# Attention: six unread products per unit on TensorE in the first five units as well

## What is computed

```python
q = jnp.transpose(q * scale, (0, 2, 1, 3))
...
q = _fq_sym(q, axis=-1)
k = _fq_sym(k, axis=-1)
v = _fq_sym(v, axis=2)
attn = jnp.einsum('bhqd,bhkd->bhqk', q, k)
attn = jax.nn.softmax(attn.astype(jnp.float32), axis=-1)
attn = _fq_unsigned(attn, axis=-1)
out = jnp.einsum('bhqk,bhkd->bhqd', attn, v)
```

## Time and profile before

| | |
|---|---|
| median of three runs | 1748.34 us (1745.9 to 1749.89) |
| profiled execution | 1749.91 us |
| its span | 1748.1 us |
| VectorE busy | 1629.3 us, 93% |
| TensorE matmuls busy | 1534.1 us, 88% |
| ScalarE busy | 1400.3 us, 80% |
| GpSimd busy | 1307.5 us, 75% |
| mean granted clock of TensorE | 0.971 |

### The profile page before, as it was taken

How to read it: one execution, slowest core, us unless ns; L and a number is a source line. 1 busy time by engine, 2 the same in 40 slices (tenths; PEclk the granted TensorE clock), 3 DMA queues, 4 the chain that set the end, 5 groups by cost and what they waited for, 6 DMA issues and landing times.

```text
span 1748.1 us, 34660 instructions
## 1 busy us (share of the span) xinstructions
PE 1534.1 (88%) x13190; PEld 752.2 (43%) x13207; DVE 1629.3 (93%) x2214; ACT 1400.3 (80%) x1354; POOL 1307.5 (75%) x1311
## 2 busy tenths in 40 slices
PE   7999968898898889889889887988888888989986
PEld 3544423444444444444444444444444444433332
DVE  6978889999999999999999999999999999588887
ACT  4578887888898888888888888987888887776874
POOL 1156737889889988988998898898998998553332
PEclk9999978999999999999999999999999998999998
DMA  7578849999868999885898999588897876314223
GB/s 243 198 255 286 282 179 172 167 186 174 153 119 143 182 175 187 177 154 107 140 186 168 179 176 158 112 148 155 151 158 144 160 138 140 79 37 97 60 68 84
DMA packets 721031, 274.22 MB, mean 157 GB/s; under 512 B 675609, under 2 KB 680281, under 8 KB 719586
## 3 DMA queue, kind: packets, MB, share of 16 engines
q1 hardware_dynamic: 719058, 268.81, 74.5%
q0 software_dynamic: 704, 1.62, 0.3%
q10 hardware_dynamic: 1104, 1.57, 0.3%
HBM read 68.21 MB, written 35.95 MB: 60 GB/s over the span
## 4 chain that ended last, share of the span: by engine, by line
DVE 48%; POOL 13%; PE 13%; issue 9%; ACT 2%; DMA 1%; POOLq 0%; DVEq 0%; ACTq 0%
DVE att_scaled L1804 46%; POOL att_probsT L1503 10%; PE att_scores L1233 3%; PE att_ps_o L1253 2%; PE att_scores L1173 2%; PE att_scores L1193 2%; POOL att_low_row L1493 1%; PE att_scores L1234 1%; ACT att_pairs L1330 1%; POOL att_bias_row L1496 1%; PE att_scores L1133 1%; DVE att_v_largest L1773 0%; PE att_ps_v L1253 0%; POOL layer_o_sum L1551 0%; DMA att_pairsT<-att_pairs 0%
## 5 line engine op out<-in xcount | busy, mean ns | idle before, releaser
L1804 DVE TENSOR_SCALAR_CACHE_REDUCE att_scaled<-att_scores,layer_nsq 128x1536 f32<-128x1536 f32 (+1 forms) x768 | 1201.2, 1637 | 13.9 <-PE att_scores L1193 10.8
L1330 ACT ACTIVATE att_pairs<-att_scaled,att_bias_row 128x4096 uint8<-128x4096 f32 x256 | 950.5, 3713 | 118.4 <-DMA att_pairsT<-att_pairs 76.3
L1503 POOL CAST att_probsT<-att_pairsT 128x2048 bf16<-128x2048 uint8 x512 | 953.6, 1891 | 95.2 <-DMA att_pairsT<-att_pairs 83.4
L1193 PE MATMUL att_scores<-first_head_area 96*128 96x512 bf16 x1024 | 297.9, 395 | 94.1 <-DVE att_scaled L1804 79.4
L1193 PE MATMUL att_scores<-att_head_area 96*128 96x512 bf16 x1024 | 289.3, 385 | 65.4 <-DVE att_scaled L1804 62.2
L1152 PEld LDWEIGHTS att_ps_o<-att_v_head,att_probsT 128*128 128x128 bf16 x8192 | 243.0, 96 | 65.0 <-issue 6.5
L1152 PE MATMUL att_ps_o<-att_v_head,att_probsT 128*128 128x32 bf16 x8192 | 245.3, 177 | 2.1 <-ACT layer_o_sum L1321 2.0
L1193 PEld LDWEIGHTS att_scores<-first_head_area 96*128 96x128 bf16 x1024 | 81.4, 99 | 255.4 <-DVE att_scaled L1804 174.9
L1193 PEld LDWEIGHTS att_scores<-att_head_area 96*128 96x128 bf16 x1024 | 79.7, 98 | 214.3 <-DVE att_scaled L1804 153.0
L1133 PE MATMUL att_scores<-att_head_area 96*128 96x512 bf16 x621 | 170.3, 384 | 0.0
L1133 PE MATMUL att_scores<-first_head_area 96*128 96x512 bf16 x570 | 158.1, 387 | 0.0
(11 more groups left out here) (192 smaller groups left out, 1596.7 us busy)
## 6 DMA issues: line engine op xcount, KB each, us to landing
layer_w2T<-ctx_T SPq DMA_DIRECT2D x96, 256.0 KB, 3.8
k_rows<-pre_shared SPq DMA_DIRECT2D x32, 392.0 KB, 2.9
pre_x_in<-in_x_dram SPq DMA_DIRECT2D x32, 256.0 KB, 4.1
kv_weights_ctx_in<-in_ctx_dram SPq DMA_DIRECT2D x32, 256.0 KB, 3.8
ctx_T<-layer_o_sum SPq DMA_DIRECT2D x8, 1024.0 KB, 5.2
pre_w_more<-in_L_ffn_w_dram SPq DMA_DIRECT2D x18, 256.0 KB, 3.4
terns<-pre_q_stage SPq DMA_DIRECT2D x32, 128.0 KB, 3.1
xb<-pre_x_in SPq DMA_DIRECT2D x16, 256.0 KB, 3.3
```

The costliest lines, as they stand in the source:

```text
L1193: last = pe.matmul(buffer[:, x:x + 512], q_head[slot][:, at:at + P], k_head[slot][:, STARTS[j] + x:STARTS[j] + x + 512], start=True, stop= ...
L1330: act.activation(pairs[g % R_BUFS][:, :].bitcast(U8).rearrange("p (c two) -> p two c", two=2), scaled[u][:, :].rearrange("p (two c) -> p t ...
L1503: pool.tensor_copy(probsT[g % C_BUFS][:, parity * HALF:(parity + 1) * HALF, :].rearrange("p k q -> p (k q)"), bytes_now.rearrange("p (n tw ...
L1804: dve.tensor_scalar(scaled[u][:, STARTS[j]:STARTS[j] + WIDTHS[j]], scores[(g * NCH + j) % 2][:, 0:WIDTHS[j]], kept["nsq"][:, g:g + 1], Non ...
```

## The change

In `step`, the condition under which the unread products are issued is widened. After j = 0 they now come in every live unit that has neither a value chunk nor early work; after j = 2 they come in every live unit that has no early work. Units 0 to 3 thus get three products in each place, unit 4 (which has a value chunk after j = 0) gets three after j = 2. In unit 0 the products after j = 0 go to columns 1024 to 1535 of `scores[1]`, ahead of chunk j = 1, which overwrites them.

```diff
@@ -1198,11 +1198,11 @@
                         elif j == 0 and live(g, UNITS):
                             if (g, j) in EARLY_PE:
                                 early_work(*EARLY_PE[g, j])
-                            elif live(g - V_LAG, UNITS):
+                            else:
                                 keep_clock(g - 1, slot, at, 3)
                         if j == 1 and live(g - V_LAG, UNITS):
                             weigh(g - V_LAG)
-                        if j == 2 and live(g - V_LAG, UNITS):
+                        if j == 2 and live(g, UNITS):
                             if (g, j) in EARLY_PE:
                                 early_work(*EARLY_PE[g, j])
                             else:
```

## The result

The changed kernel took 1760.31 us (median of four runs, 1757.39 to 1764.38), against 1749.12 us (1745.9 to 1755.44) for the kernel before beside it: ratio 1.0053, 95% interval 1.003 to 1.0077. It is slower by 0.5%, where 1746.1 us and no difference above 0.2% were forecast. A second comparison, with five runs against 17, gave 1.0082 (1.0064 to 1.0099). The profiled execution after took 1764.38 us, its span is 1762.5.

The account below looks back on a forecast made before the run. VectorE was taken to bound the kernel, with TensorE's low clock delaying it in the first five units. −3.04 + 0.8 = −2.24 us from the median 1748.34 gave 1746.1 us, range 1744.2 to 1749.6.

Parts of the forecast that it names:

- The low clock in units 0 to 4, and its price of 3.04 us: Attention's first five units: TensorE at 1.2 GHz makes VectorE wait for scores, 3.04 us over five units of 4.68.
- The clock rises within unit 0: TensorE in attention's unit 0: unbroken added products bring 2.4 GHz by about 255.5 us, instead of at 274.3.
- The added wait: VectorE's second pass in unit 0: its scores come behind the added products, a loss of 0.8 us.
- Rival 1: Units 1 to 4: clock falls again once or twice, 0.7 to 1.0 us each; time near 1747.3; chance 0.25.
- The wait at 329.53: VectorE's first wait for ScalarE in the attention, 0.49 us: it should move, not grow.
- rival 2: Gain given back where DMA is full: wait at 329.53 grows by up to 2.2 us; 1748.3 us; chance 0.10.
- by the whole gain: ScalarE at unit 4: its start follows the product with V and moves forward by all of VectorE's gain, 2.2 us.
- No wait, semaphore, DMA or pass on another engine is added: Cost of the 27 added matmuls with weight loads: only TensorE time, 0.423 us a product at the low clock.
- what follows hangs on VectorE's passes and moves with them: Rest of attention and feed-forward stage: moves with VectorE's passes, so the gain of 2.24 us is kept.
- VectorE's last pass of L1804: VectorE's pass over the scores in the attention: its last one ends about 2 us earlier.
- The spread of runs: Whole kernel: 1.5 us allowed below the largest gain and 1.3 above no gain, giving 1744.2 to 1749.6 us.
- The change's own gain: First five units: 3.04 us of waits removed less 0.8 lost, 2.24 us or 0.13% of the kernel's time.

Follow-up runs that it names:

- 27 pads: Kernel before plus 27 tiny unread 8-column products with weight loads at the end of TensorE's first stage, ahead of the attention: 1761.08 us, ratio 1.0065.
- equal boundaries: Tiny unread products ahead of attention: changed kernel plus 101 against kernel before plus 128, 0.9986 and 0.9985; plus 37 against plus 64, 0.9963 both.
- the halves: Exponentials and GpSimd casts cut to half their columns from unit 8: kernel before 1742.21 us, changed kernel 1740.88, kernel before plus 27 tiny products 1740.77.
- the change again: The changed kernel measured once more, unaltered, against the kernel before: 1765.5 us, ratio 1.0082.
- the padded kernels: Kernel before or changed kernel plus 27 to 128 tiny unread TensorE products, mostly where it idles before the attention: ratios 0.9963 to 1.0065.
- 64 pads: Kernel before plus 64 tiny unread products at the end of TensorE's first stage, half an instruction block: 1748.88 us, ratio 0.9963.

## Why the prediction was wrong

- **The low clock in units 0 to 4, and its price of 3.04 us: right.** Units 1 to 4 take 4.68 us with the change.
- **The clock rises within unit 0: right.** The products from 253.91 us on take 0.81 us for three, after work without a pause from 249.45 on. The added wait was 0.82 us, forecast 0.8; unit 5 started 2.2 us earlier since unit 0, forecast 2.24.
- **Rival 1, a falling clock in units 1 to 4: did not happen.** After the change TensorE pauses 0.83 us before 258.31 and 0.48 before 260.05, about as worked out (0.8 and 0.55), and the clock stayed at 1.00. The Trainium skill, "TensorE: Matmul & The Clock Gate", section "Why this matters for your kernels", asks for no long idle gaps between bursts of matmuls, and these units agree. The fall at 1233.3 us does not: the longest pause just ahead of it was 0.81 us. There the mechanism of this rival did occur, behind a wait for ScalarE, and is a part of the loss.
- **The wait at 329.53 and the full DMA, rival 2: right for VectorE up to there.** The wait was gone, and unit 28 was 3.2 us ahead, so the gain had even grown. But ScalarE's unit 4 had not moved "by the whole gain": a transposition held it for 0.79 us at 278.23. Rival 2 had the right stage, transpositions late in a full DMA, but knew them only as a way to lose the gain of 2.2 us, not 11 us more.
- **"No wait, semaphore, DMA or pass on another engine is added", and "what follows hangs on VectorE's passes and moves with them": this step failed.** I costed 54 instructions by their time on TensorE and left out that they have to be fetched, that the fetches are DMA packets, and that they move every later fetch against the units. The loop through a transposition had about 0.5 us of slack in two units. With the boundaries where the change puts them, more fetches fall into the later part of a transposition (70 instead of 37), and 11 us were lost; 27 pads with no other effect lose 9. VectorE's last pass of L1804 ended 13.5 us later, where I had it about 2 earlier. The sign of the result came from there.
- **The spread of runs: too small.** I took 1.5 us from three runs; the runs of one kernel spread over 5 to 25 us. The range, from 1744.2 to 1749.6, was too narrow even without the loss.
- **The change's own gain: open.** With equal boundaries the ratios are 0.9986 against 0.9985, and 0.9963 against 0.9963; with the halves 1740.88 against 1742.21. That is 0 to 0.1% where I had 0.13%, all within the intervals. With the boundaries of the change itself it even has the other sign, 1.0082 (the change again) against 1.0065 (27 pads before) in one group, also within the intervals. The 2.2 us are in the first units' timeline. In the traces with halves the start of unit 252, counted from unit 0, is 1.3 us earlier with the change than before and 3.2 earlier than with 27 pads, but these are single executions. Whether the gain reaches the end the runs can't say.

Why a fetch in the later part of a transposition delays it so much (whether it takes the turn of one of the 16 engines) was not tried. The counts in the table go with the loss but don't prove that share of it; a ScalarE that lags also moves the offsets. What the padded kernels show is that the place of the boundaries is the cause, and the halves that the way leads over ScalarE and GpSimd.

## What to carry to other kernels

An edit to one engine's program also moves the blocks in which its later instructions are fetched, and where another transfer has no slack this can be worth more than the edit. Before a small result is credited to an edit, run the old kernel with as many idle instructions, and the new one padded to a whole block. In a periodic pipeline, add up the loop that passes through a transfer (here from one exponential to the one that reuses its buffer: 8.9 of 9.36 us): if it is that tight, what shifts DMA traffic can move the time by more than the edit itself.

## What the runs showed of the hardware

- TensorE's instructions come in packets of 16384 bytes throughout the run, 105 of them on one queue, about one for every 256 instructions; with 128 matmuls more there are 106. The place of the boundaries alone moved the kernel before from 0.9963 (64 pads) to 1.0065 (27 pads) of its time.
- A fetch of 16 KB, in a stretch where it takes 2.1% of the DMA engines and the other transfers 62.7%, can go with a transposition that lands 1.8 us later than its neighbours (6.31 against 4.50 and 4.39 us).
- 54 instructions ahead of the attention cost 9 us, and 256 in the same place cost nothing that the runs show (0.9985).
- A pass held up on VectorE can cost twice: at 1233.3 us of the trace after, the granted clock fell to 0.50 after TensorE had paused 0.81 and 0.75 us behind a wait of 1.59, and VectorE then waited 0.48 us for scores.
